# First sums of a graph network: counting in 16 steps, table product and counted tiles among 24 gather steps, tile turned at a step's end

## The reference, cut to what matters

```python
sender_features = nodes[senders]
msg_in = jnp.concatenate([sender_features, edges], axis=-1)
messages = msg_in @ W_message
agg = jax.ops.segment_sum(messages, receivers, num_segments=total_nodes)
h = _layer_norm(jax.nn.relu(agg) + nodes, ln_aggr_scale, ln_aggr_bias)
nodes_out = _relu_mlp_skip(h, [mlp_W0, mlp_W1, mlp_W2], [mlp_b0, mlp_b1, mlp_b2])
nodes_new = _layer_norm(nodes + nodes_out, ln_out_scale, ln_out_bias)
...
gate_logits = x @ gate_w + gate_b
topk_vals, topk_idx = jax.lax.top_k(gate_logits, K)
```

## Time and profile before

| | us |
|---|---|
| median of 3 runs (1452.37 to 1457.22) | 1454.64 |
| the profiled execution | 1451.82 |
| its span | 1449.9 |
| TensorE busy | 1116.8 |
| GpSimd busy | 748.8 |
| VectorE busy | 740.5 |
| ScalarE busy | 550.9 |

### The profile page before, as it was taken

The page is one execution under the profiler, slowest core; times in us unless marked ns, Lnnn a source line. Parts: engine busy times, 40 slices in busy tenths (PEclk is TensorE's granted clock), DMA queues, the critical chain, the costliest instruction groups (busy, mean ns, idle before and its releaser), DMA issues. The chain is left out here.

```text
span 1449.9 us, 27321 instructions
## 1 busy us (share of the span) xinstructions
PE 1116.8 (77%) x7233; PEld 955.9 (66%) x7234; DVE 740.5 (51%) x2520; ACT 550.9 (38%) x1632; POOL 748.8 (52%) x844
## 2 busy tenths in 40 slices
PE   1389988988997379999993767738888897498870
PEld 0278888887887279999992333327767786387660
DVE  7245776766656721111113899837766244733335
ACT  3565565655223234444443555440000001344330
POOL 6677777777300042222224677457657772077770
PEclk9999998999999689999997799965589895689995
DMA  5655555555300169999993222153333442433237
GB/s 180 168 150 148 144 150 145 147 147 141 88 12 14 71 219 311 352 352 350 348 347 115 66 88 90 49 162 109 98 93 113 117 118 68 135 110 96 94 98 269
DMA packets 186770, 220.02 MB, mean 152 GB/s; under 512 B 69103, under 2 KB 148503, under 8 KB 186382
## 3 DMA queue, kind: packets, MB, share of 16 engines
q1 hardware_dynamic: 148240, 125.81, 27.1%
q0 software_dynamic: 32352, 87.30, 20.7%
q10 hardware_dynamic: 6046, 5.40, 1.2%
HBM read 187.33 MB, written 32.19 MB: 151 GB/s over the span
## 5 line engine op out<-in xcount | busy, mean ns | idle before, releaser
L775 POOL DMA_INDIRECT O0G<-n_rows,src_tab x260 | 253.0, 973 | 92.4 <-issue 87.6
L775 POOL DMA_INDIRECT O1G<-sparse_rows,src_tab x188 | 180.2, 958 | 79.8 <-issue 62.4
L1956 POOL DMA_INDIRECT e0xs<-token_rows,e0idx x60 | 57.0, 950 | 161.6 <-ACT e0idx L2042 160.9
L2093 DVE TENSOR_TENSOR e0ys<-e0ps_y,NR 128x256 f32<-128x256 f32 x64 | 27.2, 425 | 217.6 <-PE e0ps_y L2015 217.6
L794 PE MATMUL O0ps_sums<-O0OH,O0G 128*128 128x80 f32 x1040 | 131.9, 282 | 1.6 <-DMA O0G<-n_rows,src_tab 1.4
L794 PEld LDWEIGHTS O1ps_sums<-O1OH,O1G 128*128 128x128 f32 x752 | 118.7, 245 | 17.6 <-issue 15.2
L794 PE MATMUL O1ps_sums<-O1OH,O1G 128*128 128x80 f32 x752 | 119.4, 328 | 13.0 <-DMA O1G<-sparse_rows,src_tab 7.0
L794 PEld LDWEIGHTS O0ps_sums<-O0OH,O0G 128*128 128x128 f32 x1040 | 125.9, 198 | 4.4 <-issue 2.8
L2001 PE MATMUL e0ps_h<-e0xT,e0W 128*128 128x128 f32 x1024 | 128.1, 279 | 0.0
L2001 PEld LDWEIGHTS e0ps_h<-e0xT,e0W 128*128 128x128 f32 x1024 | 122.8, 196 | 0.1
L2015 PE MATMUL e0ps_y<-e0W,e0hidT 128*128 128x256 f32 x512 | 120.9, 379 | 0.0
(11 more groups left out here) (378 smaller groups left out, 2493.0 us busy)
## 6 DMA issues: line engine op xcount, KB each, us to landing
e0W<-in_L_ffn_w SPq DMA_DIRECT2D x128, 512.0 KB, 5.8
O0EA<-in_edge_attr SPq DMA_DIRECT2D x97, 128.0 KB, 3.1
expert_out<-e0ys SPq DMA_DIRECT2D x64, 128.0 KB, 5.3
O0G<-n_rows,src_tab POOLq DMA_INDIRECT x260
e1W_all<-in_L_ffn_w SPq DMA_DIRECT2D x16, 256.0 KB, 5.6
n_rows<-NR SPq DMA_DIRECT2D x5, 640.0 KB
token_rows<-O0N SPq DMA_DIRECT2D x25, 128.0 KB, 2.7
m0own<-token_rows SPq DMA_DIRECT2D x25, 128.0 KB, 2.2
```

What stands on the lines that cost most here:

```text
L775: pool.indirect_dma_start(out=self.G[:, s, k, :], out_offset=None, in_=self.rows_dram, in_offset=bass.IndirectOffsetOnAxis(ap=src_tab[:, g ...
L1956: pool.indirect_dma_start(out=xs[:, s, :], out_offset=None, in_=token_dram, in_offset=bass.IndirectOffsetOnAxis(ap=idx[:, s:s + 1], axis=0 ...
```

## The change

- The units are counted in steps 0 to 15: five a step in the first five, 41 in the other eleven. The new `quarter` splits a step's units and pieces evenly over its four places.
- There are 24 gather steps. The first has four gathered groups, the others share 61. The near groups lie in steps 0 to 18.
- Tiles 24 to 7 enter first, then 2, 1 and 0, then 6 to 3, one a step from step 1 (`AHEAD` is 1): the last at step 25, 31 steps in all. The pieces lie in steps 16 to 20. Groups 33 to 35, which reach into tile 2, move ahead of it; from step 19 on, only groups from 36 up are left, and the flag's limits say so.
- At each place a group comes first and a unit behind it, alternating.
- The turn of `H` and the copy to `hT` move from the beginning of lag 2 to the end of lag 1: on TensorE behind the logits, on ScalarE behind the second relu. ScalarE's `group(3)` moves behind both.

```diff
-    AHEAD = 2
+    AHEAD = 1
...
-    GATHER_STEPS = 22
+    GATHER_STEPS = 24
+    FIRST_GATHERS = 4
+    UPPER_FIRST = 18
+    DENSE_AT = UPPER_FIRST + AHEAD
...
+        nodes = list(range(T - 1, T - 1 - UPPER_FIRST, -1)) + list(range(DENSE_TILES - 1, -1, -1)) + list(range(T - 1 - UPPER_FIRST, DENSE_TILES - 1, -1))
+        far, near, border = (list(range(n - 1, low - 1, -1)) for n, low in ((NG, CLEAR_GROUP), (DENSE_GROUPS, 0), (CLEAR_GROUP, DENSE_GROUPS)))
+
+        def far_by(u):
+            return min(u, 1) * FIRST_GATHERS + (NG - DENSE_GROUPS - FIRST_GATHERS) * max(u - 1, 0) // (GATHER_STEPS - 1)
+
+        far[far_by(DENSE_AT) - len(border):far_by(DENSE_AT) - len(border)] = border
...
-    UNIT_STEPS = GATHER_STEPS - 1
-    FIRST_PASS_BY, PASSES_BY = plan0.step_of(T - DENSE_TILES), plan0.step_of(T - 1)
+    UNIT_STEPS, RAMP, RAMP_UNITS = 16, 5, 25
+    FIRST_PASS_BY, PASSES_BY = (plan0.step_of(plan0.nodes.index(t)) for t in (DENSE_TILES - 1, 0))
...
-            return round(UNITS * min(n, UNIT_STEPS) / UNIT_STEPS)
+            if n <= RAMP:
+                return RAMP_UNITS * n // RAMP
+            return RAMP_UNITS + round((UNITS - RAMP_UNITS) * (min(n, UNIT_STEPS) - RAMP) / (UNIT_STEPS - RAMP))
         return range(by(u), by(u + 1))
+
+    def quarter(of_step, q):
+        return of_step[len(of_step) * q // 4:len(of_step) * (q + 1) // 4]
...
                         if adjacency:
-                            for v in parts(units_of(u), q):
-                                adjacency.count(pe, v)
-                            for i in parts(pieces_of(u), q):
+                            groups, units = parts(groups_of(u), q), quarter(units_of(u), q)
+                            for j in range(max(len(groups), len(units))):
+                                for o in groups[j:j + 1]:
+                                    sums.products(pe, o)
+                                for v in units[j:j + 1]:
+                                    adjacency.count(pe, v)
+                            for i in quarter(pieces_of(u), q):
                                 adjacency.piece(pe, i)
...
-                        for o in parts(groups_of(u), q):
-                            sums.hot_and_add(dve, o)
+                        groups, units = parts(groups_of(u), q), quarter(units_of(u), q) if adjacency else ()
+                        for j in range(max(len(groups), len(units))):
+                            for o in groups[j:j + 1]:
+                                sums.hot_and_add(dve, o)
+                            for v in units[j:j + 1]:
+                                adjacency.add(dve, v)
...
                 group(0)
-                if x := at(2):
-
-                    t, s = x
-                    wait_tile(act, S["turned"], t)
-                    for k in range(K2):
-                        last = nc.scalar.activation(self.hT[:, s, k, :], self.ps_tn[:, k * P:(k + 1) * P], ACT.Identity,
-                                                    bias=aggr_cols[:, 1, k:k + 1], scale=aggr_cols[:, 0, k:k + 1])
-                    last.then_inc(S["hT_ready"], 1)
...
-                group(3)
                 if x := at(2):
                     wait_tile(act, S["second"], x[0])
                     relu(1, self.ps_01, x[0], S["relu1"])
+                if x := at(1):
+                    t, s = x
+                    wait_tile(act, S["turned"], t)
+                    for k in range(K2):
+                        last = nc.scalar.activation(self.hT[:, s, k, :], self.ps_tn[:, k * P:(k + 1) * P], ACT.Identity,
+                                                    bias=aggr_cols[:, 1, k:k + 1], scale=aggr_cols[:, 0, k:k + 1])
+                    last.then_inc(S["hT_ready"], 1)
+                group(3)
...
-                if x := at(2):
-                    t, s = x
-                    wait_tile(pe, S["h_ready"], t)
-                    wait_tile(pe, S["hT_ready"], t, 1)
-                    turn2(self.ps_tn, self.H[:, s, :], S["turned"])
                 group(0)
...
+                if x := at(1):
+                    t, s = x
+                    wait_tile(pe, S["h_ready"], t)
+                    wait_tile(pe, S["hT_ready"], t, 1)
+                    turn2(self.ps_tn, self.H[:, s, :], S["turned"])
                 group(3)
```

More of the change, by code:

```diff
@@ L27 @@
 DENSE_GROUPS = 33
+CLEAR_GROUP = 36
 DENSE_TILES = 3
@@ L86, in base_limit @@
         def base_limit(self, g):
-            done = [t for t, u in zip(self.nodes, self.starts) if t >= self.lowest and self.groups_before(u) <= self.sequence.index(g)]
+            done = [t for t, u in zip(self.nodes, self.starts) if t >= max(self.lowest, DENSE_TILES) and self.groups_before(u) <= self.sequence.index(g)]
             return min(done) * P - WINDOW if done else NPAD
@@ L397, in _ @@
                 for c in range(CHUNKS):
-                    kinds.append((DENSE_GROUPS + sum(MORE_GROUPS[:c]), MORE_SPAN, MORE_LOW[c] + MORE_W - MORE_SPAN,
-                                  MORE_LOW[c] - 1 + MORE_SPAN, P + 1, -MORE_LOW[c]))
+                    first = DENSE_GROUPS + sum(MORE_GROUPS[:c])
+                    for g, low in ((first, MORE_LOW[c]), (CLEAR_GROUP, DW)):
+                        if g == first or first < g < first + MORE_GROUPS[c]:
+                            kinds.append((g, MORE_SPAN, MORE_LOW[c] + MORE_W - MORE_SPAN, low - 1 + MORE_SPAN, P + 1, -MORE_LOW[c]))
                 cols = (span_col, room_col, low_col, wide_col, off_col)
@@ L1254, in group @@
                                 more.piece(pe, i)
-                        for o in parts(groups_of(u), q):
-                            sums.products(pe, o)
+                            for o in parts(groups_of(u), q):
+                                sums.products(pe, o)
                     return group
@@ L1331, in group @@
                             def group(q):
-                                for v in parts(units_of(u), q) if adjacency else ():
+                                for v in quarter(units_of(u), q) if adjacency else ():
                                     adjacency.hot(act, v + 1)
```

12 lines of the change are left out of this document (5 added, 7 removed).

## The result

| | before | after |
|---|---|---|
| median of 4 runs, us | 1453.51 | 1472.51 |
| lowest and highest | 1450.7, 1457.22 | 1463.48, 1476.64 |
| profiled execution | 1451.82 | 1476.64 |
| its span | 1449.9 | 1474.7 |

The account below looks back on a forecast made before the run. Gather steps were taken as bound by TensorE and VectorE handing work to each other, VectorE the fuller. Stretch times put the first-sums stage's end at 500.2 instead of 492.8, 7.4 us later: 1462 against the 1454.6 median; range 1446 to 1476.

Parts of the forecast that it names:

- much slower: Rival: sums' product waits over 1.7 us every step, matmuls behind it at half clock; 1476 us, chance 0.13.
- the turn: Steps 5 to 15: first layer's 14.6 us of waits go, a wait at the sums' product replaces them; no gain taken.
- Start: Before tile 0 enters: one step with five units and five groups, entry at 78 us (74 to 82), before 86.92.
- steps 16 to 23: TensorE full, table product hides behind nothing: 95 us for steps 16 to 20, 37 (34 to 41) for 21 to 23.
- step 24: Last step before tile 24 enters, without groups: 8 us, entry at 466 against 453.93 before.
- 5.1 us for a tile: TensorE's cost of one tile, used to sum steps 16 to 20 to 95 us.
- Tail: After tile 24 enters: VectorE's three relu waits and one us of slow matmuls go, 38.9 us becomes 34.2.
- Steps 1 to 4: Tile 0 to tile 4, seven more units mostly in VectorE's idle time: 59 us (55.3 to 68.6), before 55.3.
- Steps 5 to 15: Tile 4 to tile 15, seven more units cost 13.3 us on VectorE: 189 us (178 to 200), before 175.65.
- 161 us: VectorE's estimated busy time plus gaps in the kernel before's steps 5 to 15, of 175.7 us.
- the wait at the lhs copy: TensorE at the sums' product waits for ScalarE's lhs copy, its chain 1.9 us longer by a fourth-quarter unit.
- faster: Rival: the layer's wait goes, none replaces it, clock stays up, VectorE works through; 1445 us, chance 0.22.

Follow-up runs that it names:

- e12: Changed kernel with VectorE's additions of counted units at fixed table columns instead of columns read into registers (counts land wrong): 1429.1 us, ratio 0.9886.
- e3: Changed kernel with its 66 units spread evenly over the 16 steps instead of five a step first: 1469.3 us, ratio 1.0155.
- e4: Kernel before with only the turn of H and the copy to hT moved to the end of lag 1: 1433.6 us, ratio 0.9894.
- e8: Changed kernel with units spread evenly over 18 steps and the kernel before's order within the places on both engines: 1472.4 us, ratio 1.0140.
- e5: e4 plus the changed kernel's order within the places and even split over the four places, units still over 21 steps: 1468.4 us, ratio 1.0110.
- e6: e5 with the 66 units in 16 steps instead of 21, nothing else: 1455.2 us, ratio 1.0031.
- e1: Changed kernel with TensorE taking the count first and the group's product behind it at each place: 1478.0 us, ratio 1.0201.
- e9: Changed kernel with, on VectorE alone, the groups' additions first and the units behind them at each place: 1477.1 us, ratio 1.0164.
- e10: Changed kernel with three unread filler products on TensorE ahead of the second group's product in the fourth place, steps 4 to 15: 1471.7 us, ratio 1.0130.
- e11: e4 with the units over 22 steps, exactly 3 a step and none in the fourth place; table product in steps 22 to 25: 1433.3 us, ratio 0.9860.

## Why the prediction was right or wrong, point by point

The side was right and 1472.5 lies inside the range (1446 to 1476), but near its upper end: outside the 1457 to 1468 that had most of the chance, and nearer to "much slower" (1476) than to the forecast (1462). The loss was forecast as 7.4 us and is 19. One term was mis-sized, and a second was right in size for a wrong reason: the gain of the turn was put at nothing, and what stands against it was put too low. That these two partly hid each other is luck.

- **Start, steps 16 to 23, step 24:** 78.9, 97.1, 37.0 and 8.0 against 78, 95, 37 and 8. TensorE is busy 94.7 of 97.1 us in steps 16 to 20; that the table product hides behind nothing was right. The 5.1 us for a tile don't come out of the row that I gave: (64.1 - 32 - 8) / 5 is 4.8, which makes the sum 93. The last gather starts at 453, after 400 as said. The stages behind took 4 us less, which is within what runs differ by.
- **Tail:** 38.9 before, 34.2 forecast, 37.1 measured, all to the start of the next stage. VectorE's three waits for the relu, which I had go altogether (3.65 us), became 0.42 us each.
- **Steps 1 to 4, the term that was mis-sized:** 59 forecast, 70.5 measured, above my upper bound of 68.6. I stayed at the lower end because VectorE was busy only 39.5 of 80.2 us. That row leaves out VectorE's gaps, which I had counted one paragraph earlier, and it begins two steps too early. In before's own steps 1 to 4 VectorE was busy 29.6 us and idle 18.4 ahead of the 13 units, 48 of 55.3; in after 33.5 and 29.6 ahead of 20 units, 63 of 70.5 (6.5 and 21.6 of these gaps are towards the count, so partly waiting). That "the gathers set the pace" there isn't in the trace: TensorE's waits in before's steps 1 to 4 are 5.8 us for a unit's addition and 0.2 for a group's, none for a gather. e12 without the registers took 59.0: my 59 would have been right for units that read none. The two units in the fourth place of each of these steps, which I hadn't priced, come on top (e3).
- **Steps 5 to 15:** 189 forecast, 193.0 measured, inside the bounds. The size held, the reason only partly. That a counted unit is dear because of its registers is what e12 shows (29 us of this stretch); that the stretch is a sum of 1.9 us a unit is not so: four more units cost 2 us (e3), seven more under the old order 19 us (e4 to e8), and with the old number the new places alone make it 197 (e5, in an execution 11 us above its median). Counted from e4's 167.7 us, the seven units and the new places together cost 25 and not 13; the 8 us that the turn gives and I didn't take made up for most of that.
- **The turn, "so I take no gain here":** refuted. It is worth 16 us in the kernel before and 21 in the changed one. The step that failed is the one from "VectorE is the fuller one" to no gain. The 161 us themselves hold: in e4 the same sum is 121.8 + 29.8 + 2.8, and the estimated 8, 162 of 167.7. But 161 of 175.7 left 14.7 us, in them 7.5 in which VectorE waited for a count that stood behind the layer's wait, and these went with the turn. I had them before me in the earlier trace rows and took the fuller engine for a full one. And the wait at the lhs copy was sized by kind, not by length: 6.5 us in e4, never above 0.8.
- **The rival "faster" (1445)** is what the turn alone does, and more (1433.6). **"Much slower" (1476)** is nearest by its number, not by its mechanism: it forecast half-clock matmuls behind each lhs wait; eight of the eleven long waits stood elsewhere, at a group's product behind a unit's addition. I had not read the order at the border of two steps on the two engines side by side. That a wait of about 1.5 us decides isn't so: in after's steps 5 to 15 one of 1.41 us had a gathered product of 1.98 us behind it and another of 1.41 one of 3.38.
- **The signs:** tile 15 later than 320, the last gather after 400, the new wait at the sums' product and none at the first layer came true. Tile 4 came in at 149.4 and not before 142, two of steps 16 to 20 lie outside 17 to 21 us (15.3 and 21.5), and VectorE was busy 125.5 of 193.0 us, 0.65 and not over 0.78 (my own sum gave 121.6 + 7 x 0.87 = 128 of 189, 0.68). So it isn't VectorE's busy time that sets the pace.
- **The balance:** from e4 to after the rest of the change costs 39 us: order and places +35 (e5), 16 instead of 21 steps for the units -13 (e6), tiles, pieces and 24 steps +14 (e3), the five units a step at first +3, less than runs differ. By the ratios it is 34: +31, -11, +18 and -4. These hold in this sequence alone: e1, e8 and e9 show that undoing the order in the changed kernel gives nothing back.
- **Clock:** after's 0.88 against 0.95 seems to cost little by itself (e10, which brought it back in these steps).

Left open: why order and load don't add up, that is why the new order with 34 units in steps 5 to 15 (e5), the old one with 41 (e8) and the new one with 41 or 45 all end at 17 to 18 us a step. What they share, and the 15 us steps of e4 and e11 don't, is a unit in the fourth place of most steps; a run of e5 with its three units in the first three places would test that and wasn't made. All these kernels read registers ahead of each unit; whether e5's cost, too, goes without them wasn't tried. A third bank for the groups' products might take away the wait at them directly. It wasn't tried either: the stage holds eight banks, and two users of one bank would have to be ordered by further waits. The Trainium skill, "PSUM — Partial Sum Buffer", section "PSUM bank collisions raise a hardware error", says why unordered sharing is no way out; no run here shows it.

## What to carry to other kernels

When two engines wait for each other, the fuller one isn't yet a full one: ask what its waits for the other hang on before you say that taking a wait from the other gains nothing, and test the move alone. A stall of 1 us ahead of an instruction on the shared path hides under other names in the rows: after's row without a releaser said 29.3 us, and without the stall the kernel was 43 us faster, so look for it before reordering. Changes that came together should be measured apart: here one part was worth 16 us and lay hidden under 35 us of another.

## What the runs showed of the hardware that was not expected

- Reading two base registers ahead of VectorE's additions costs about 1 us of idle VectorE (32.6 us ahead of 34 units in e4), and taking it away for 66 units made the kernel 43 us faster, 0.66 us a unit, although VectorE was busy only 125 of 193 us.
- In the records of the changed kernel a wait of 2.63 us had a product of 3.67 us behind it, one of 1.54 us in e10 had 1.98, which is full speed; of two waits of 1.41 us in the changed kernel one had 1.98 behind it and one 3.38. Filling some of the waits raised the granted clock of the stretch from 0.88 to 0.95 and left the time where it was.
